# A cross-attention and feed-forward kernel: a rebuilt prologue, and every key tile weighted by three split products instead of four tiles in twelve by one full-precision product

## The reference

```python
# x (8, 56, 128), ctx (8, 1500, 96); 8 heads of 64
q = layernorm(x) @ Wq;  k = ctx @ Wk;  v = ctx @ Wv
sim = einsum('bihd,bjhd->bhij', q, k) * 64 ** -0.5
out = einsum('bhij,bjhd->bihd', softmax(sim), v)
x = x + out @ Wout + bout
# feed-forward, with activations and weights rounded to int8 steps
xq = fake_quant(layernorm(x))
h = fake_quant(silu(xq @ quant(w_gate).T) * (xq @ quant(w_up).T))
x = x + h @ quant(w_down).T
```

## Time and profile before

| | us |
|---|---|
| three runs: lowest, median, highest | 196.88, 198.62, 201.15 |
| the profiled execution | 199.18 |
| its span, from the first to the last instruction | 197.4 |
| busy in the span: PE, DVE | 188.5, 144.1 |
| busy in the span: ACT, POOL | 114.3, 103.9 |

### The profile page before, as it was taken

The page is one execution under the profiler, slowest core; times in us unless marked ns, Lnnn a source line. Parts: engine busy times, 40 slices in busy tenths (PEclk is TensorE's granted clock), DMA queues, the critical chain, the costliest instruction groups (busy, mean ns, idle before and its releaser), DMA issues.

```text
span 197.4 us, 2704 instructions
## 1 busy us (share of the span) xinstructions
PE 188.5 (95%) x867; PEld 143.9 (73%) x867; DVE 144.1 (73%) x331; ACT 114.3 (58%) x240; POOL 103.9 (53%) x94
## 2 busy tenths in 40 slices
PE   8599998999999999999999999999999999999883
PEld 2496565888877888778888888888887888866431
DVE  2417979886987788488869866989698618946674
ACT  3035685756576576556765746576666365744231
POOL 5864859265655645466546534755565267460120
PEclk9757999999999999999999999999999999999999
DMA  6973472005201410151034104210010000000001
GB/s 153 198 165 106 126 198 75 2 0 150 87 0 28 167 41 0 18 178 40 0 83 130 28 0 113 91 32 0 0 39 0 3 0 2 0 2 3 0 0 47
DMA packets 11638, 11.38 MB, mean 58 GB/s; under 512 B 8288, under 2 KB 9488, under 8 KB 11624
## 3 DMA queue, kind: packets, MB, share of 16 engines
q1 hardware_dynamic: 10824, 10.38, 19.9%
q10 hardware_dynamic: 800, 0.83, 2.1%
HBM read 10.96 MB, written 0.23 MB: 57 GB/s over the span
## 4 chain that ended last, share of the span: by engine, by line
PE 85%; DVE 6%; DMA 3%; ACT 2%; issue 1%; POOL 1%; POOLq 0%; SPq 0%; DVEq 0%; ACTq 0%
PE p_o L820 12%; PE p_m L785 11%; PE p_s L803 9%; PE p_s L798 9%; PE p_s L799 9%; PE p_o L832 7%; PE p_o L827 7%; PE p_o L829 6%; DMA wqT<-wqT_d 3%; PE p_x L838 3%; PE p_m L763 2%; PE p_s L877 2%; PE p_o L877 1%; PE p_x L846 1%; ACT silu L439 1%
## 5 line engine op out<-in xcount | busy, mean ns | idle before, releaser
L305 POOL TENSOR_TENSOR e_lo<-e_full,e_hi 125x448 fp32r<-125x448 f32 x64 | 82.0, 1283 | 65.0 <-ACT e_full L406 64.7
L504 DVE TENSOR_REDUCE chunk_max<-p_m 112x1 f32<-112x500 f32 x96 | 63.9, 675 | 29.6 <-PE p_m L785 27.0
L404 ACT ACTIVATE e_hi<-p_s 125x448 fp32r<-125x448 f32 x64 | 34.9, 546 | 35.0 <-PE p_s L803 34.0
L798 PE MATMUL p_s<-q_hi,ctxT_lo 96*125 96x448 f32 x96 | 45.9, 478 | 0.0
L785 PE MATMUL p_m<-ctxT_hi,q_hi 96*112 96x500 f32 x96 | 37.9, 414 | 0.9 <-DVE chunk_max L504 0.9
L803 PE MATMUL p_s<-q_hi,ctxT_hi 97*125 97x448 f32 x96 | 35.4, 369 | 0.0
L799 PE MATMUL p_s<-q_lo,ctxT_hi 96*125 96x448 f32 x96 | 35.1, 365 | 0.0
L406 ACT ACTIVATE e_full<-p_s 125x448 f32<-125x448 f32 x64 | 34.4, 538 | 0.0
L820 PE MATMUL p_o<-e_full,ctx_nat 125*128 125x448 f32 x64 | 29.4, 540 | 0.0
L409 ACT ACTIVATE e_full<-p_s 125x448 f32<-125x448 f32 x32 | 17.4, 544 | 16.8 <-PE p_s L803 16.8
L827 PE MATMUL p_o<-e_hi,ctx_hi 125*128 125x448 f32 x64 | 23.9, 373 | 0.0
(11 more groups left out here) (187 smaller groups left out, 209.9 us busy)
## 6 DMA issues: line engine op xcount, KB each, us to landing
ctxT_in<-ctxT_d SPq DMA_DIRECT2D x8, 562.5 KB, 4.7
ctx_in<-ctx_d SPq DMA_DIRECT2D x8, 375.0 KB
ctx_nat<-ctx_d SPq DMA_DIRECT2D x8, 187.5 KB
q_hi<-maxima SPq DMA_DIRECT2D x28, 0.4 KB, 1.9
wqT<-wqT_d SPq DMA_DIRECT2D x1, 256.0 KB, 6.1
wout<-wout_d ACTq DMA_DIRECT2D x1, 256.0 KB, 9.6
x_in<-x_in_d SPq DMA_DIRECT2D x1, 224.0 KB, 2.9
wkT<-wkT_d ACTq DMA_DIRECT2D x1, 192.0 KB, 3.7
```

What stands on the lines that cost most here:

```text
L305: pool.tensor_tensor(e_lo[:, k, :], e_full[:, k, :], e_hi[:, k, :], ALU.subtract)\
L404: act.activation(e_hi[:, k, :], p_s[n % 2][0:KT, 0:HQ], ACT.Exp, scale=SCALE)\
L504: dve.reduce_max(chunk_max[:, c // NM, c % NM:c % NM + 1], p_mb[c % NM][0:GQ, 0:MC], AX.X)\
L798: pe.matmul(o, ctxT_lo[b % 2][:, keys], q_hi[0:C, b, :], start=True, stop=False)
```

## The change

**The native tiles go.** All 12 tiles are split: PE makes three fp32r products for each, and `ctx_nat`, its DMAs and constants are gone; `ctx_in`, `ctx_hi` and `ctx_lo` are 12 tiles wide instead of 8 (a half is 576 columns instead of 384). For 10 tiles in 12 POOL makes `e_lo` as before. For t of 5 and 11 ACT writes the full exponentials not to SBUF but to the PSUM bank `p_x`, and DVE subtracts `e_hi` from there (`e_lo_from_psum`), one tile later.

**DVE's order changes.** `maxima` follows its chunk at once; the four steps of the normalisation stand at t = 3, 4, 5, 6, `ctx_lo` at t = 7 and 8, the second layer norm at t = 9. `p_x` is now shared with `project`, which waits for the subtraction at t = 6, and with the product for `wvo`, which moves from batch 0 to batch 1.

**The prologue is rebuilt.** x, wqT and wkT come in parts, the head weights lie on 128 partitions instead of 64, the first transposed context comes in three DMAs, and the loads of wvT, wout and the biases move behind the first contexts. The first layer norm is made for the first pair of batches alone; the first maxima are taken over three banks in one reduction of 1500 numbers (`first_max`); POOL takes over two thirds of the first `ctxT_hi`, and `ctx_hi` of batch 0; ACT takes `ctxT_hi` of batch 1. Two of the eight query products move into slots 1 and 2 of the loop. Seven filler products stand at the start instead of 11, and five later instead of one.

```diff
-NATIVE = (2, 5, 8, 11)
+LO_DVE = (5, 11)
+LO_POOL = tuple(t for t in range(T) if t not in LO_DVE)
...
 # ScalarE, exponentials of tile n
-                if t in SPLIT:
-                    act.activation(e_hi[:, k, :], p_s[n % 2][0:KT, 0:HQ], ACT.Exp, scale=SCALE)\
-                        .then_inc(s.exp_made, 1)
+                act.activation(e_hi[:, k, :], p_s[n % 2][0:KT, 0:HQ], ACT.Exp, scale=SCALE)\
+                    .then_inc(s.exp_made, 1)
+                if t in LO_POOL:
                     act.activation(e_full[:, k, :], p_s[n % 2][0:KT, 0:HQ], ACT.Exp, scale=SCALE)\
                         .then_inc(s.exp_made, 1)
                 else:
-                    act.activation(e_full[:, k, :], p_s[n % 2][0:KT, 0:HQ], ACT.Exp, scale=SCALE)\
-                        .then_inc(s.exp_made, 2)
+                    act.activation(p_x[0:KT, 0:HQ], p_s[n % 2][0:KT, 0:HQ], ACT.Exp, scale=SCALE)\
+                        .then_inc(s.exp_made, 1)
...
 # VectorE
+            def e_lo_from_psum(n):
+                k = n % RING
+                dve.wait_ge(s.exp_made, 2 * n + 2)
+                dve.tensor_tensor(e_lo[:, k, :], p_x[0:KT, 0:HQ], e_hi[:, k, :], ALU.subtract).then_inc(s.lo_dve_made, 1)
...
+                    if t == LO_DVE[0] + 1:
+                        e_lo_from_psum(T * b + LO_DVE[0])
+                    if b and t == 0:
+                        e_lo_from_psum(T * b - 1)
-                    if t in (3, 4, 6, 7) and b:
+                    if 3 <= t <= 6 and b:
                         normalise(b - 1, (b - 1) % 2, t - 3)
-                    if t in (5, 7) and b + 1 < B:
-                        split_ctx_lo(b + 1, (t - 5) // 2)
+                    if t in (7, 8) and 0 < b < B - 1:
+                        split_ctx_lo(b + 1, t - 7)
...
                 if b == B - 1:
                     quantise_weights()
+                    e_lo_from_psum(T * B - 1)
...
 # TensorE, weighted(n)
-                if t in NATIVE:
-                    j = NATIVE.index(t)
-                    pe.matmul(o[:, 0:HQ], ctx_nat[b % 2][:, j, :], e_full[:, k, :], start=(t == 0), stop=(t == T - 1),
-                              skip_group_check=True).then_inc(s.pv_done, 1)
-                    return
+                if t in LO_POOL:
+                    pe.wait_ge(s.lo_made, splits_before(n) + 1)
+                else:
+                    pe.wait_ge(s.lo_dve_made, 2 * b + LO_DVE.index(t) + 1)
...
 # TensorE, project(p)
                 pe.wait_ge(s.attn_made, 2 * p + 2)
+                pe.wait_ge(s.lo_dve_made, 2 * (2 * p + 2) + 1)
...
 # SyncE, the first loads
-            sp.dma_start(x_in[:, :, :], x_d).then_inc(s.x_loaded, 16)
-            sp.dma_start(wqT[:, :, :], wqT_d).then_inc(s.qk_loaded, 16)
-            load_ctxT(0)
-            sp.wait_ge(s.qk_loaded, 32)
+            sp.dma_start(x_in[:, 0, :], x_d[:, 0, :]).then_inc(s.x0_loaded, 16)
+            sp.dma_start(wqT[:, 0:2, :], wqT_d[:, 0:2, :]).then_inc(qk_loaded[0], 16)
+            sp.dma_start(wqT[:, 2:HP, :], wqT_d[:, 2:HP, :]).then_inc(qk_loaded[1], 16)
+            sp.dma_start(x_in[:, 1:PAIRS, :], x_d[:, 1:PAIRS, :]).then_inc(s.x_loaded, 16)
+            sp.wait_ge(qk_loaded[0], 32)
+            for k in range(NM):
+                sp.dma_start(ctxT_in[0][:, key_piece(k)], ctxT_d[0, :, key_piece(k)]).then_inc(first_ctxT_loaded[k], 16)
+            sp.wait_ge(first_ctxT_loaded[0], 16)
```

542 lines of the change are left out of this document (326 added, 216 removed).

## The result

The changed kernel takes 204.92 us (median of 4 runs, 202.65 to 205.97) against 198.97 us of the kernel before on the same chip: 1.028 times as long, with a 95% interval of 1.018 to 1.038, so it is slower, while a loss of 2% or more isn't settled. The forecast was 193.3 us, its range 189.0 to 199.5. The profiled execution took 204.72 us, with a span of 202.9 against 197.4.

A forecast was written before the change was run, and what follows sets the result against it. PE was taken to bound the kernel, 85% of the span. Terms -4.5 + 1.8 + 2.4 + 0.9 - 7.2 + 1.3 = -5.3 took the span from 197.4 to 192.1, giving 193.3 us beside 198.62; range 189.0 to 199.5.

The forecast's parts named there:

- The prologue: Ahead of the loop: the loop would begin at 18.5 us instead of 25.66, -7.2 us; bounds 16.8 and 21.5.
- On the way it waits: Prologue step: PE waits for the first context's pieces, POOL's copies and the first maxima; 1.8 us left for such waits.
- the second rival's: The clock stays low: PE's new gaps keep it at 1.2 GHz, 195.8 us; chance 0.13 together with a DMA delay.
- DVE: In the loop: DVE, with more work and waits for POOL, comes late and holds three projections, +2.4 us (0 to 5).
- the last tile: End of the loop: `e_lo` of tile 95 comes late behind the weights' quantisation on DVE, +0.9 us (0 to 3).
- in the mean 0.5, 2.5 a batch: Five DVE instructions a batch can meet POOL, each waiting 0 to 1.05 us, in the mean 0.5.
- slower than before: Rival: DVE and POOL hold each other up, small instructions of residual and layer norm wait too; above 206 us, chance 0.06.
- `project`: In the loop: three projections wait for DVE's `attn`, 0.8 us each, 2.4 us in all (0 to 5).
- The maxima themselves may come 3 us late before PE waits: In the loop: DVE's maxima have 3 us to spare, so they aren't the place where PE feels DVE's lateness.
- the native tiles: In the loop: splitting 32 native tiles saves PE 0.14 us each, -4.5 us (4.2 to 4.8).
- ACT's place: In the loop: PE newly waits about 0.3 us for the last piece of `ctxT_hi` in six batches, +1.8 us.
- The two queries and the moved `wvo`: Two queries paid in slots 1 and 2 of the loop, +1.3 us; the `wvo` products only move from batch 0 to 1.

The follow-up runs named there:

- Experiment 1: The changed kernel with DVE's layer norm of the other three pairs ahead of the first chunk's maximum instead of behind it: 198.99 us, ratio 0.996.
- experiment 4: The changed kernel with POOL subtracting only 8 of 448 columns of each of its tiles, so its instructions are short: 195.23 us, ratio 0.984.
- experiment 10: The kernel of 9 with DVE subtracting tile 5 ahead of the chunk's maximum and tile 95 ahead of the weights' casts: 188.41 us, ratio 0.953.
- kernel 7: The changed kernel with layer norm ahead of the first chunk, last `ctxT_hi` third at t = 10, `rstd2` after tile 4, weights quantised in batch 7: 192.98 us.
- the isolated rows: Separate kernels running rows of DVE instructions beside POOL's subtractions, without the computation; a DVE subtraction begun beside the first of three queued on POOL took 1.49 us.
- experiment 5: The changed kernel with POOL's `rstd2` in batches 3, 5 and 7 after the subtraction of tile 4 instead of tile 1: 202.85 us, ratio 1.023.
- 2: The changed kernel with the last third of `ctxT_hi` made by ACT at t = 10 instead of 11: 201.21 us, ratio 1.012.
- 9: kernel 7 with the projection at t = 9, quantisation except maxima and scales behind the loop, and `ctx_lo` at t = 8 and 10: 190.92 us, ratio 0.954.

## Why the prediction was wrong

**What bounds the kernel** was read rightly for before, and one test of it was named ("as long as no other engine comes late"). That condition failed.

**The prologue** is the first step that failed: -7.2 us became -1.0. The step was "On the way it waits", a list of DMAs, POOL's copies and the first maxima. It left out that the other three pairs' layer norm is DVE's as well, that its place in DVE's queue is behind the first chunk, and that the queries, most of PE's remaining work, hang on it. Experiment 1 shows it: these instructions in front are worth 3.6 us. The other 2.6 of the missing 6.2 go with the slow first products, which no term had. The terms it had were sound: the first product came at 4.03 us (predicted 4), and with the four instructions in front the loop began at 17.8 to 18.4, or at 21.1 and 21.2 with slow first products, against 18.5 and a bound of 21.5. The fall of the clock was the second rival's, but as a consequence of these gaps.

**DVE** is the second step, a term mis-sized: +2.4 and +0.9 for the lateness and the last tile, where experiment 4 measured 7.3 + 2.1 = 9.4 us for all meetings with POOL, some 1.6 of it the clock. Of "in the mean 0.5, 2.5 a batch" the size was right and the end of the range and the count weren't. For `ctxT_lo` it held (1.19 us in the mean of 21 against 0.67 alone), but a wait was 2.0 where POOL had no gap, and I had set an upper end of 1.05. The meetings are more than five: `rstd2`, the small instructions of layer norm 2 (1.12 and 1.06 instead of 0.2 and 0.16) and the quantisation wait too. POOL is shut out as well, which packs its queue for the next meeting. Without the meetings the loop is 2.4 us shorter than before (experiment 4), where the sum without its term for DVE has 1.4. The rival "slower than before", with a chance of 0.06, had this mechanism, and one of its places, the second layer norm; the residual's instructions took what they take in experiment 4, but for one copy (0.55 instead of 0.23 us). That the result lies near its 206 is luck: it put 20 us on DVE, where 9.4 were measured, and kept the -7.2 of the prologue, which was -1.0. Its own numbers, 20 in place of 2.4, also give 211 and not 206.

**`project`** was expected 0.8 us late three times; it was 0.1 in batch 2, 1.7 and 2.7 in batches 4 and 6. The last one includes about 1 us of the clock, 0.50 for about 3 us behind the gap; I had charged no wait with what it does to the clock. These 4.5 us lie within the 0 to 5 given. The rest of the 7.3 came at places that the sum didn't have: 0.8 twice for `e_lo` of tile 5 in batches 3 and 5, 0.3 twice for the row of maxima, 0.6 for the clock in the slot behind the last projection. "The maxima themselves may come 3 us late before PE waits" was refuted too: their row's DMA held PE twice, 0.3 us a slot.

**Right, or nearly:** the native tiles (batch 3 of experiment 10, without a wait, takes 17.47 us against 18.03, so 0.14 a tile); ACT's place (0.39 against 0.3, in four batches of the kernel after and in all six of experiment 4; the exponential written to PSUM took 0.54 us, as those to SBUF); the new subtraction, 611 to 625 ns in all 16; nothing in the loop from POOL's own load. The two queries and the moved `wvo` cost 0.2 us instead of 1.3: batches 0 and 1 together took 37.6 us against 38.1, of which the eight native tiles are -1.1 and `ctxT_hi` +0.4.

**The range** ended at 199.5. The loop's start, 24.7, lies outside its bound of 21.5, and the 7.3 us outside the 0 to 5 given for DVE in the loop; only the rival that the range left out reached 205.

## What to carry to other kernels

Where work is handed to an engine, list every instruction of that engine's queue from the first to the last that PE hangs on, the ones that are not moved too, and ask of each what stands in front of it. Where DVE and POOL both work on SBUF, price a meeting at the whole of the other's instruction (0.9 us here for one column as for 448), and bear in mind that the loop showed two in a row, which the isolated rows didn't; a lateness of one slot is then met not by less work but by room, such as the projection one slot later or two subtractions that don't stand side by side. Eight changes of place took this kernel from 204.9 to 188.4 us with the same work.

## What the runs showed of the hardware

PE's first products came in two kinds, with the profile's granted clock at 1.00 in both: the two fillers near 6 to 7 us took 0.60 us together in some executions and 1.06 in others, for instance (kernel 7, then the kernel after):

```profile
5.90 0.60 PE L853 MATMUL p_n<-filler 128*128 128x512 bf16 x2
```
```profile
7.02 1.06 PE L851 MATMUL p_n<-filler 128*128 128x512 bf16 x2
```

The second filler of such a pair begins 0.43 us after the first in the slow kind and 0.22 us in the other. The seven fillers before 4.1 us took 3.17 us in both, so both begin slowly; it ended near 6 us in experiment 5 and at about 10.9 in the kernel after and in experiments 1, 2 and 9. What decides isn't known. The rest that I hadn't expected stands above: waits of DVE for two instructions of POOL in a row (2.67 us, in the loop alone), POOL kept out by a ctx_lo that began 0.43 us after it (2.16 instead of 1.13 us), and that this depends on what DVE ran ahead of the reductions in front of that ctx_lo.
